# Causal attention in a decoder kernel: one sum of the four key tiles' weights on GpSimd in place of per-tile products with ones

## What is computed

```python
def _attention(x, wq, wk, wv, wo):          # HQ = 16 heads, K = V = 64
    ...                                      # q, k turned by rotary tables, 4 key heads shared
    scores = jnp.einsum('btghk,bThk->bghtT', qg, k)
    mask = jnp.tril(jnp.ones((t, t), bool))
    scores = jnp.where(mask, scores, -jnp.inf) / np.float32(np.sqrt(K))
    p = jax.nn.softmax(scores, axis=-1)
    out = jnp.einsum('bghtT,bThv->btghv', p, v).reshape(b, t, HQ * V)
    return out @ wo
```

## Time and profile before

| | |
|---|---|
| median of 3 runs | 1944.27 us (1944.12 to 1945.07) |
| the profiled execution | 1946.76 us, of which the span 1945.0 us |
| PE busy over the span | 1534.9 us (79%) |
| DVE busy | 1097.1 us (56%) |
| ACT busy | 643.5 us (33%) |
| POOL busy | 136.1 us (7%) |
| the stage touched | first score product at 699.93 us, last output multiplied at 880.89 us |

### The profile page before, as it was taken

How to read it: one execution, slowest core, us unless ns; L and a number is a source line. 1 busy time by engine, 2 the same in 40 slices (tenths; PEclk the granted TensorE clock), 3 DMA queues, 4 the chain that set the end, 5 groups by cost and what they waited for, 6 DMA issues and landing times. The chain is left out here.

```text
span 1945.0 us, 22922 instructions
## 1 busy us (share of the span) xinstructions
PE 1534.9 (79%) x8440; PEld 713.2 (37%) x8440; DVE 1097.1 (56%) x2729; ACT 643.5 (33%) x906; POOL 136.1 (7%) x162
## 2 busy tenths in 40 slices
PE   1797759994768799995997997984988559995874
PEld 0332334441224344445443333352436423333342
DVE  4695444446964667763444872545445465744345
ACT  1365332223325023330443662421212125551431
POOL 1000000001000510000000000000000012331000
PEclk9898769996969789997997997996987779997797
DMA  4000000003000010000002000000010000000000
GB/s 192 1 1 1 1 1 0 1 0 127 1 1 1 1 44 1 1 2 1 1 0 95 1 1 0 1 1 0 0 65 1 1 1 1 2 2 1 1 1 11
DMA packets 4078, 27.33 MB, mean 14 GB/s; under 512 B 384, under 2 KB 2432, under 8 KB 2944
## 3 DMA queue, kind: packets, MB, share of 16 engines
q1 hardware_dynamic: 2912, 25.35, 3.3%
q10 hardware_dynamic: 1056, 0.52, 0.1%
HBM read 25.35 MB, written 0.52 MB: 13 GB/s over the span
## 5 line engine op out<-in xcount | busy, mean ns | idle before, releaser
L628 DVE TENSOR_REDUCE maxima<-banks 128x1 f32<-128x512 f32 (+4 forms) x640 | 362.9, 603 | 109.7 <-PE banks L499 102.1
L758 ACT ACTIVATE big<-banks 128x1024 f32<-128x1024 f32 (+2 forms) x320 | 294.3, 960 | 285.1 <-PE banks L542 114.4
L527 PE MATMUL banks<-big 32*128 32x512 f32 (+6 forms) x1280 | 234.5, 617 | 17.5 <-DVE big L649 12.7
L499 PE MATMUL banks<-big 32*128 32x77 bf16 (+6 forms) x1024 | 152.8, 296 | 21.0 <-ACT big L234 6.1
L563 PE MATMUL banks<-big,v_heads 128*9 128x512 f32 (+7 forms) x1024 | 159.6, 569 | 6.1 <-ACT heads_out L693 3.2
L342 POOL TENSOR_TENSOR rstd<-mean_var,minus_half 128x4 f32<-128x4 f32 x46 | 46.9, 1019 | 1583.5 <-DVE mean_var L317 1583.5
L1144 ACT ACTIVATE big<-banks 128x512 f32<-128x512 f32 (+1 forms) x120 | 71.5, 596 | 200.4 <-PE banks L1114 200.4
L1169 DVE TENSOR_TENSOR big<-big,banks 128x512 f32<-128x512 f32 (+1 forms) x88 | 60.4, 686 | 130.2 <-PE banks L1117 125.1
L1127 PE MATMUL banks<-big,moe_weights 128*128 128x512 f32 (+1 forms) x240 | 123.0, 593 | 2.8 <-DVE big L1166 1.5
L499 PEld LDWEIGHTS banks<-big 32*128 32x128 bf16 (+1 forms) x1024 | 56.6, 97 | 170.7 <-DVE maxima L628 83.8
L527 PEld LDWEIGHTS banks<-big 32*128 32x128 f32 (+3 forms) x1280 | 73.7, 179 | 67.6 <-ACT big L758 26.9
(11 more groups left out here) (379 smaller groups left out, 2286.9 us busy)
## 6 DMA issues: line engine op xcount, KB each, us to landing
moe_weights<-in_moe SPq DMA_DIRECT2D x1, 4896.0 KB, 22.3
moe_weights<-in_moe SPq DMA_DIRECT2D x1, 4864.0 KB, 15.0
moe_weights<-in_moe SPq DMA_DIRECT2D x1, 3264.0 KB, 10.7
moe_weights<-in_l3x SPq DMA_DIRECT2D x1, 3072.0 KB, 10.0
late_weights<-in_l2x SPq DMA_DIRECT2D x1, 2048.0 KB, 8.1
moe_weights<-in_l SPq DMA_DIRECT2D x1, 1234.0 KB, 13.2
rows<-in_rows SPq DMA_DIRECT2D x1, 1152.0 KB, 8.1
late_weights<-in_turned SPq DMA_DIRECT2D x1, 1152.0 KB, 17.3
```

Of the source, the lines that this page charges most:

```text
L499: last = nc.tensor.matmul(RING[n % NR][:, x * klen:x * klen + last_key(t)], q[rows, t * P:(t + 1) * P], ks[rows, 0:last_key(t)], start=Tru ...
L527: last = nc.tensor.matmul(SC[pair % 2][0:size, j % 2, n0:S], ks[rows, i * P:i * P + size], q[rows, n0:S], start=True, stop=turned)
L628: nc.vector.tensor_reduce(dst, src, AX_X, ALU.max).then_inc(ring_free.up(), 1)
L758: nc.scalar.activation(E[pair % NEP][0:size, :, n0:S], SC[pair % 2][0:size, :, n0:S], ACT.Exp, scale=scale).then_inc(exp_ready.up(), 1)
```

## The change

It applies where `HB` is 2 and there are several key tiles, which is this stage alone (`added_up`).

- GpSimd adds up the exponentials of a group's four tiles in one buffer `added` (2 x 512 columns, the storage of the masked weights, not in use here): after round 1 of a group a copy of the first 128 queries' weights of tile 0 and an addition of tiles 0 and 1, after round 2 an addition of tile 2, after round 3 one of tile 3. Before the first it waits until PE has used the buffer for the group before (`den_ready`).
- PE makes two products with ones per group (`added_sums`), 512 wide, in round 1 of the next group, after the values. Those of even groups go to the places 0 and 32 of `DEN`, those of odd ones to 64 and 96. The eight products of `sums` are gone.
- ACT copies `DEN` to `OT` once for two groups (`move_sums`), in round 2 after the second; in `move_out` only the copy of the output is left. PE's transposes of the sums then happen once for two groups, in round 3 of an even group, after the 128-wide raw units; the two spreads of the inverses follow each other in round 1 of the odd group after it.
- DVE takes the reciprocal straight from the bank, and then spreads it twice; the copy and the small reduction (L668, L669) are gone.
- An exponential now waits for GpSimd as well before it overwrites a weight buffer.

```diff
-    per_batch = 2 if halved and nkt == 1 else 1
+    added_up = halved and nkt > 1
+    per_batch = 2 if halved else 1
     batch_rounds = per_batch * nkt
-    later = 5 if nkt > 1 else 4
+    turn_after = 4 if added_up else 3
+    later = turn_after + (2 if nkt > 1 else 1)
...
+    def additions(r):
+        return r // nkt * (nkt - 1) + max(r % nkt, 1)
...
+    def added_sums(pe, g):
+        pe.wait_ge(added.sem, added.at((g + 1) * (nkt - 1)))
+        if g == 0:
+            pe.wait_ge(cleared.sem, cleared.at(1))
+        if g and g % 2 == 0:
+            pe.wait_ge(den_moved.sem, den_moved.at(g // 2))
+        for j in range(HB):
+            at = 64 * (g % 2) + 32 * j
+            last = nc.tensor.matmul(DEN[at:at + 32, :], c.ones[:, 0:32], c.added[:, j, :], start=True, stop=True)
+        last.then_inc(den_ready.up(), 1)
...
     def turn_sums(pe, s):
...
+        if added_up:
+            pe.wait_ge(den_moved.sem, den_moved.at(s + 1))
+        else:
+            pe.wait_ge(out_moved.sem, out_moved.at((s + 1) * per_batch))
...
-        if halved and nkt > 1:
-            rc = c.RC[:, s % 2, :, 0:HB]
-            parts = tr.rearrange("p t (x j) w -> p t j x w", x=2)[:, :, :, :, 0]
-            nc.vector.tensor_copy(rc[:, 0], parts[:, 0, :, 0])
-            nc.vector.tensor_reduce(rc[:, 1:], parts[:, 1:], AX_X, ALU.add).then_inc(ring_free.up(), 1)
-            dve.wait_ge(ring_free.sem, ring_free.at(n + 1))
-            seq(dve, dve_step, nc.vector.reciprocal(rc, rc))
-        else:
-            rc = c.RC[:, s % 2]
-            nc.vector.reciprocal(rc, tr[:, :, :, 0]).then_inc(ring_free.up(), 1)
-            dve.wait_ge(ring_free.sem, ring_free.at(n + 1))
+        rc = c.RC[:, s % 2]
+        nc.vector.reciprocal(rc, tr[:, :, :, 0]).then_inc(ring_free.up(), 1)
+        dve.wait_ge(ring_free.sem, ring_free.at(n + 1))
...
+    def move_sums(act, s):
+        act.wait_ge(den_ready.sem, den_ready.at((s + 1) * per_batch))
+        if s >= 2:
+            act.wait_ge(ring_free.sem, ring_free.at(sums_turned[s - 2] + 1))
+        nc.scalar.copy(OT[:, s % 2, :], DEN[:, :]).then_inc(den_moved.up(), 1)
...
                 if 0 <= r - 1 < R:
                     sums(pe, r - 1)
-                if summed(r - 3) is not None:
-                    turn_sums(pe, summed(r - 3))
+                if added_up and ended(r - 2) is not None:
+                    added_sums(pe, ended(r - 2))
+                if summed(r - turn_after) is not None:
+                    turn_sums(pe, summed(r - turn_after))
...
+            for r in range(R if added_up else 0):
+                g, i = r // nkt, r % nkt
+                w, first, total = E[r % NEP], start(i), c.added
+                if i == 0:
+                    continue
+                pool.wait_ge(exp_ready.sem, exp_ready.at(r + 1))
+                if i == 1:
+                    if g:
+                        pool.wait_ge(den_ready.sem, den_ready.at(g))
+                    whole = E[(r - 1) % NEP]
+                    nc.gpsimd.tensor_copy(total[:, :, 0:first], whole[:, :, 0:first])
+                    nc.gpsimd.tensor_tensor(total[:, :, first:], whole[:, :, first:], w[:, :, first:], ALU.add).then_inc(added.up(), 1)
+                else:
+                    pool.wait_ge(added.sem, added.at(g * (nkt - 1) + i - 1))
+                    nc.gpsimd.tensor_tensor(total[:, :, first:], total[:, :, first:], w[:, :, first:], ALU.add).then_inc(added.up(), 1)
```

More of the change, by code:

```diff
@@ L436, in row_attention @@
     (ring_ready, ring_free, negmax_ready, score_ready, exp_ready, value_ready, out_moved, inverse_ready, masked_ready, cleared, room_cleared,
-     projected, project_free, dve_step) = (counter(c, n) for n in (
+     projected, project_free, dve_step, added, den_ready, den_moved) = (counter(c, n) for n in (
          "ring_ready", "ring_free", "negmax_ready", "score_ready", "exp_ready", "value_ready", "out_moved", "inverse_ready",
-         "masked_ready", "cleared", "room_cleared", "projected", "project_free", "dve_step"))
+         "masked_ready", "cleared", "room_cleared", "projected", "project_free", "dve_step", "added", "den_ready", "den_moved"))
     filled, emptied = itertools.count(), itertools.count()
@@ L467, in last_use @@
     def last_use(r):
-        return r + 2 if halved and r % 2 == 0 else r + 1
+        return r + 2 if halved and not added_up and r % 2 == 0 else r + 1
+    def additions(r):
+        return r // nkt * (nkt - 1) + max(r % nkt, 1)
     def place(g):
@@ L565, in values @@
                 nc.tensor.matmul(out[:, 0:i * P], vop(b, HB * k + j, i), e[:, 0:i * P], start=first, stop=False, skip_group_check=True)
-        if turned or halved and r % 2 == 0:
+        if turned or added_up or halved and r % 2 == 0:
             last.then_inc(value_ready.up(), 1)
+    def added_sums(pe, g):
[8 more added lines that the diff above has]
+        last.then_inc(den_ready.up(), 1)
     def sums(pe, r):
@@ L571, in sums @@
         b, k = groups[g]
+        if added_up:
+            return
         if halved and r % 2:
@@ L600, in turn_sums @@
         sums_turned[s] = n
-        pe.wait_ge(out_moved.sem, out_moved.at((s + 1) * per_batch))
+        if added_up:
+            pe.wait_ge(den_moved.sem, den_moved.at(s + 1))
+        else:
+            pe.wait_ge(out_moved.sem, out_moved.at((s + 1) * per_batch))
         if n >= NR:
@@ L689, in move_out @@
         act.wait_ge(value_ready.sem, value_ready.at((g + 1) * nkt))
+        if added_up:
+            nc.scalar.copy(place(g), OV[:, :]).then_inc(out_moved.up(), 1)
+            return
         if s >= 2:
@@ L747, in _ @@
                 empty(act, project_bank(n)).then_inc(project_free.up(), 1)
-            for r in range(R + 2):
+            for r in range(R + 3):
                 if ended(r - 2) is not None:
                     move_out(act, ended(r - 2))
+                if added_up and summed(r - 3) is not None:
+                    move_sums(act, summed(r - 3))
                 if r >= R:
@@ L757, in _ @@
                         act.wait_ge(value_ready.sem, value_ready.at(last_use((pair - NEP) // pairs)))
+                        if added_up:
+                            act.wait_ge(added.sem, added.at(additions(pair - NEP)))
                     nc.scalar.activation(E[pair % NEP][0:size, :, n0:S], SC[pair % 2][0:size, :, n0:S], ACT.Exp,
@@ L780, in _ @@
                     move_negmax(dve, next_group(r))
-                if summed(r - 3) is not None:
-                    invert_sums(dve, summed(r - 3))
+                if summed(r - turn_after) is not None:
+                    invert_sums(dve, summed(r - turn_after))
                 for u in rest:
@@ L1989, in decoder @@
         c.EM = [EM[:, i * 2 * P:(i + 1) * 2 * P].rearrange("p (x t) -> p x t", x=2) for i in range(4)]
+        c.added = EM[:].rearrange("p (x t) -> p x t", x=2)
         c.OT = c.sb("heads_out", [P, 2 * S])[:].rearrange("p (z t) -> p z t", z=2)
```

## The result

| | before | changed |
|---|---|---|
| median | 1944.45 us (4 runs, 1944.12 to 1945.07) | 1959.86 us (4 runs, 1955.21 to 1960.14) |
| ratio | | 1.0073, 95% interval 1.0056 to 1.0091 |
| profiled execution, span | 1946.76, 1945.0 us | 1960.14, 1958.3 us |
| stage, first score product to last multiplication | 180.96 us | 193.55 us |

12.6 of the 13.3 us by which the spans differ lie in the stage. A group is called even or odd by its number, counted from 0.

A forecast was written before the change was run, and what follows sets the result against it. PE's queue sets the stage's pace, partly racing DVE. PE's order and the stage's end gave -3.6 us, GpSimd's blocks +4.0, total +0.4 on a median of 1944.27: 1944.7 us, range 1937.5 to 1952.5.

The forecast's parts named there:

- order on PE: PE's removed, added and moved work with its waits for DVE, plus the stage's end: 3.6 us less in all.
- end of the stage: After the last group's start: the final sums hang on GpSimd, so 14.44 us becomes 15.3, a loss of 0.9.
- GpSimd's blocks: At DVE's negated maxima, L642 waits for GpSimd's running addition: 0.35 us per even group, 0.1 per odd, 4.0 in all.
- A: First score product to issue of the 512-wide raw scores: from 5.93 us to 5.97 (even group) or 7.09 (odd).
- B: Issue of the 512-wide raw scores to transposes of the negated maxima: from 4.25 us to 2.88 without a block.
- C: Transposes of the negated maxima to the next group: 1.01 us in odd groups, 2.03 in even ones.
- the price of the added products: PE's two 512-wide float32 products per group: taken as 1.00 us.
- rival 3: Expected waits in PE's groups don't appear and its own saving comes through whole: 1932 us, 8% chance.
- GpSimd's own time: GpSimd's copy and additions per group: 4.5 us with gaps, hidden unless they take twice as long.
- rival 4: GpSimd is twice as slow on the strided sums and becomes the bound, 12 us a group: 1957 us, 5% chance.
- rival 1: GpSimd doesn't block L642, DVE's 8-column operation on the negated maxima: 1940.7 us, 30% chance.
- rival 2: L641 and L642 both block, one after the other, GpSimd's last addition slipping in between: 1952 us, 14% chance.

The follow-up runs named there:

- e6: The changed kernel with GpSimd's additions shrunk to a few columns and four unused transposes before PE's wait for the negated maxima: ratio to before 0.9982, 1941.8 us.
- e4: The changed kernel with eight unused transposes on PE before its wait for the negated maxima: ratio to before 1.0012, 1948.8 us.
- e9: The changed kernel run once more, unaltered: ratio to before 1.0082, 1959.4 us.
- e1: The changed kernel with every GpSimd addition shrunk to a few columns, all orders and waits kept: ratio to before 0.9991, 1945.0 us.
- e3: The changed kernel with the two added products, and ACT's copy of the sums, one round later: ratio to before 1.0071, 1959.4 us.
- e2: The kernel before plus the change's four GpSimd instructions per group, their sum unused, ACT waiting for them: ratio to before 1.0046, 1952.6 us.
- e8: The changed kernel with two buffers for GpSimd's sums, the added products left in place: ratio to before 1.0079, 1958.3 us.

## Why the prediction was wrong

Forecast 1944.7 (1937.5 to 1952.5), measured 1959.9, outside the range. Two terms of the sum failed: the granted clock, which it holds at nothing without a reason, and the blocks, which it puts at half their size. In the stage, step by step:

| step | forecast us | measured us |
|---|---|---|
| order on PE, end of the stage included | -3.6 | -4.2 (e6 against before, without the start's 1.3) |
| GpSimd's blocks | +4.0 | +8.6 (e4 against e6, its 0.5 at the stage's end included) |
| granted clock | 0, not considered | +8.2 (changed against e4, without the start's 1.3) |

The three measured terms make the 12.6 us by which the stage grew (before and the changed kernel start at the lower clock, e4 and e6 at the higher one, so the 1.3 us cancel). They are differences of single executions, by my estimate good to 1 or 2 us: with e9 in place of the changed kernel, which starts at the higher clock as e4 does, the clock's term is 193.46 - 184.04 = 9.4. The end of the stage is split between the rows: it was forecast at +0.9 and measured +0.4 in the first row (14.86 against 14.44 us) and +0.5 in the second.

**What bounds the stage, and the order on PE: right.** A, B without a block and C came out within 0.1 us, and so did the price of the added products. That the removed work is paid back by waits for DVE, so that 0.88 us per group doesn't come off, is what e1 and e6 show (rival 3 is out). One number in it doesn't follow from its own terms: PE's idle time before L512 without a block. PE comes 1.57 us earlier and B shrinks by 1.37, so 0.24 grows to 0.44, not to "about 0.6"; e1 has 0.45 on average. GpSimd's own time was right too: 0.40 + 1.86 + 1.26 + 0.72 = 4.2 us in a group, as forecast without the gaps, hidden (rival 4 is out); PE waits for it only at the end of the stage, 0.65 us.

**The block: right in kind, half in size** (rival 1 is out). The step that failed is "in an odd group the last addition at about 9.9, so by 0.1". I had laid out GpSimd's time once, for the even group, and used it for both. In an odd group the two spreads push rounds 2 and 3 back by 1.1 us, and with them the exponentials that the additions wait for. The last addition then starts just ahead of L664, which is as late for the same reason, and the block is 0.48 us instead of 0.1. In even groups it was 0.58 against 0.35: there L663 was held, which I had given to rival 2, and L664 still had to run behind it. Rival 2, both blocked one after the other, didn't occur in this kernel (in e3 it does, by another GpSimd instruction for each); its time (1952) was nearer than the forecast only by chance, since its mechanism wasn't what happened.

That a block was in the sum at all rests on less than the prediction says. Its row for it, L679 at 1657.01, ends 0.29 us after the GpSimd product; unhindered, with its 0.43, it would have ended 0.23 after it. A delay of 0.06 us doesn't show that it waited for the end. The rows of this change do: an instruction of 0.20 us ends 0.05 us after the addition, whichever addition it is.

The Trainium skill, SBUF — State Buffer (Who interferes with whom), names more than I took from it: besides instructions with two SBUF inputs, `copy` and `tensor_scalar` can enter a two-port mode, if their operands allow it, and can then contend with GpSimd as well. The runs agree with both: L663 is a `tensor_scalar` from SBUF to SBUF and waited 0.58 us, L664 has two SBUF inputs and waited 0.48 us (1.56 in e3), while the 512-wide reductions from PSUM kept their 0.69 us beside GpSimd's additions. L679, which the prediction gives for the first kind, is a copy with one SBUF input, so by the page it could be of the second only.

**The clock: missing.** I wrote that PE's idle time before L512 would grow from 0.24 to 0.6 to 1.0 us, and priced it as idle time only. What the engine does afterwards belonged into the sum: in the changed kernel the scores product at the head of an odd group takes 2.08 us (at 756.00) or 1.51 (at 781.17) instead of 1.13, wholly or partly at the 1.2 GHz level. e4 shows that this hangs on what PE does in that gap and not on anything GpSimd does: PE gets useless work in that place, nothing else changes, and the clock stays at 1.00. e1 shows the same from the other side: GpSimd does next to nothing, and the clock falls. What it costs is 1.2 to 2.3 us in five of the six odd groups of the middle, and up to 0.5 in even ones.

**Open.** How much idle time it takes, and whether idle time is the right measure. The profiled execution of e2 idles 0.75 us before its negated maxima are turned, in each group but the first, and keeps 1.00; e1 idles 0.45 us there on average and falls to 0.94. Nor does the idle time of whole groups put the two in order: at clock 1.00 a group of e2 leaves PE idle for 1.11 us, one of e1 for 1.33 (even) and 0.63 (odd), 0.98 on average. They also differ in the work done (948 against 822 products in the same 120 us), and two of e2's six executions were 8 us longer at a lower mean clock. No run here separates these. I can say that filling the gap is enough, in e4 and e6, and not what the least filling would be, nor whether it acts as filled time or as added work. Nor did I try to keep DVE's two steps clear of GpSimd in another way, or shorter additions.

## What to carry to other kernels

A small operation on the path can pay for a long one on an "idle" engine: before moving work to GpSimd, lay its instructions beside every DVE instruction that reads and writes SBUF, in each kind of group separately, and look above all at the short ones for which another engine waits. When work is taken off an engine that is paced by a race, ask what it will wait for next, and what its clock does while it waits; put what is left of its work where it would wait. Here the later products and the second buffer together turned a loss of 0.7% into a gain of 0.7%, with the same instructions.

## What the runs showed of the hardware

- A DVE instruction of 8 columns, 0.18 to 0.20 us alone, takes up to 1.76 us when a GpSimd addition or copy of SBUF data is running; it ends 0.04 to 0.06 us after that instruction, in all 15 groups of the changed kernel and in e2, e3, e4 and e8. GpSimd's additions of 256 and 512 columns took 0.72 to 0.73 and 1.26 to 1.28 us whether an instruction waited for them or not.
- The granted clock of TensorE fell to the 1.2 GHz level for parts of groups in kernels in which PE stood still before L518 for 0.45 us on average (e1) or 1.0 (the changed kernel), out of some 11; with 0.75 (e2) it held in the profiled execution. Four (e6) or eight (e4) unused float32 transposes in that gap kept it at 2.4 GHz.
- GpSimd's copy of 128x256 took 0.40 us, its addition of 128x768 1.80 to 1.86 us, where 1.80 had been put from the smaller ones.
- Two float32 products of 512 columns at two 32-partition places took 0.98 us; four at four places, two of 512 and two of 384 columns, had taken 0.99.
